# A fused decoder layer with routed experts: the first expert rows are issued behind three weight loads, and the last batch's routing moves one pipeline step

## The chip, the cores and the metric

The kernel runs on one core of one Trainium2 chip. The metric is device microseconds (us) of one execution, the median over runs. The engines are named PE (TensorE, matrix multiplies), DVE (VectorE), ACT (ScalarE), POOL (GpSimd) and SP (SyncE, which here only issues DMAs).

## What is computed

The reference takes `x` of 4 batches x 512 positions x 128 channels in float32 and adds three blocks to it, each behind a layer norm:

```python
x = x + _L0_attn_ref(_layernorm(x), ...)            # gated Toeplitz mixer over four positions
x = x + _L0_xattn_ref(_layernorm(x), ctx_1024, ...) # 16 heads of linear attention on a context of 77
x = x + _L0_ffn_ref(_layernorm(x), router_w, w_gate, w_up, w_down)
```

The third is a mixture of 8 experts, of which each of the 2,048 tokens takes two:

```python
logits = xf @ router_w.T
top_w, top_i = lax.top_k(softmax(logits), 2);  top_w = top_w / top_w.sum(-1)
g, u = xf @ w_gate[e].T, xf @ w_up[e].T        # 128 -> 256, for each expert e
y = (silu(g) * u) @ w_down[e].T                # 256 -> 128
out = sum over the two chosen experts of top_w * y
```

Only the chosen experts need be computed. The layer norm in front of it, the logits, the choice of experts and the combination are all part of the kernel.

## The kernel before

The engines run five instruction streams written out by hand, with semaphores between them. There are three stages one after the other: the mixer, the attention (16 heads on each of four batches of 512 tokens) and the experts.

**Routing.** For each batch m, `third_norm(m)` normalises the tokens into the tile `rows` (128 partitions x 2 choices x 4 tiles x 130 numbers: 128 channels, a token number and a weight). It has a POOL part (`var_eps`, then `rstd`, lines 517 to 523) and a DVE part (line 927). `turn_rows` (PE, line 1038) transposes the rows, `turned_rows` (ACT) copies them to `y3T`, and `router_logits` (PE, line 1187) multiplies them by the router. `routing(m)` is a list of eight DVE pieces: top two of the logits (945, 949), one-hot masks (953, 957), differences (960, 961), then `slots`, `places` and `weights` (965 to 979). `ranks` (PE, lines 1194 to 1202) counts the tokens in front of each token for its expert. `scatter(m, t)` (POOL, line 537) then writes 128 rows to the DRAM tensor `dispatched` (`xs`), at the place of their expert: 4 tiles x 2 choices are eight indirect DMAs for a batch, each adding 16 to the semaphore `sent`.

For batches 0 to 2 all this lies in the attention of the next batch. For batch 3, the last, there is no next attention, so it lies beside the first experts.

**The table of blocks.** The tokens of an expert are cut into blocks of 128. `table_steps` are small DVE steps which turn the counts (`base`) into a table of blocks: where each block's rows start, and so which expert it is. This is done twice: an early table of 16 blocks, built from the first three batches alone (semaphore `table_step` reaches 11), and a late table of 24, with the last batch in it (reaches 32). 39 blocks are run in all.

**Experts.** A block s is loaded by SP: `load_weights(s)` brings the 256 KB of gate and up weights of its expert into one of 8 buffers (`wgu_sb`, line 378) and `load_rows(s)` its 128 rows (65 KB) into one of 16 buffers (`xb`, line 372). `read_rows` reads four or more table entries into SP registers ahead of that (line 367). Rows may be loaded only when the batches they come from have been scattered: SP waits for `sent` of three batches ahead of block 0, and of all four ahead of block 16. Weights of block s from 8 on wait for the gate and up product of block s - 8.

`pipeline(engine, stages, beside)` runs the blocks as software pipeline steps. At step j, PE turns the rows of block j (`turn_x`, line 1242), multiplies block j - 1 by its gate and up weights (`gate_up`, line 1250) and block j - 2 by its down weights (`down`, line 1260). ACT copies the turned rows of block j (line 574), takes the silu of the gate of block j - 1 (`gate`, line 682) and weighs the result of block j - 2 (`weigh`, line 686, tile `yo`). DVE multiplies gate and up (`hidden`, line 1013, block j - 1, tile `hid`). POOL sends the result of block j - 2 by an indirect DMA to `expert_out` (`send`, line 557). Work named under `beside` is written out behind the stages of its step. PE enters this pipeline when DVE is through with all heads of the last batch but one.

After block 38, SP loads `expert_out` back (`y_back`), DVE adds it to X (line 1029) and SP stores X. Each of these waits for every send.

Of the kernel before, what the change touches and what calls it, by code (L numbers as in the profile page):

```python
# [21 lines left out]
NB = 4  # L22
POS = 512
TPB = POS // P
# [20 lines left out]
WRING = 8  # L45
AHEAD = 4
# [11 lines left out]
def decoder_kernel(nc, x, ctxT, wuv, bu, bv, woaT, bo, coef, wk, wv, wq, wo, projT, router, wgu, wd,  # L58
                   out, xs, ys):
    with ExitStack() as ctx:  # L60
# [203 lines left out]
        CONSTS = 18 + RING  # L264

        WARM = 6
        PE_MIXER, PE_Y2, ACT_Y2, DVE_Y2, POOL_LN2 = 2, 6, 6, 3, 2
        POOL_NORM = 3
        SCATTER = (10, 11, 12, 13)
# [33 lines left out]
        def pipeline(eng, stages, window=None, beside=None, late=None, moved=()):  # L303

            depth = max(lag for lag, _ in stages)

            def tick(i, j):  # L310
                for lag, fn in stages:
                    s = i * RING + (j - lag)
                    if 0 <= s < RUN and (fn, s) not in moved:
                        fn(s, (j - lag) % RING, i + (j - lag) // RING, *((j - lag,) if window else ()))
            for i in range(BLOCKS // RING):
                if late and i == EARLY // RING:
                    late()
                if window:
                    window(i)
                for j in range(RING):  # L320
                    tick(i, j)
                    for step in (beside or {}).get(i * RING + j, ()):
                        step()
            if window:
                window(BLOCKS // RING)
            for j in range(depth):
                tick(BLOCKS // RING, j)


        @block.sync  # L330
        def _(sp):
            for g in range(NG):
                part = slice(G // 2 * g, G // 2 * (g + 1))
                sp.dma_start(wk_sb[:, part, :], wk[:, part, :]).then_inc(ld_wk[g], 16)
            for i in range(2):
                part = slice(G * i, G * (i + 1))
                sp.dma_start(wv_sb[:, part, :], wv[:, part, :]).then_inc(ld_wvo[i], 16)
                sp.dma_start(wo_sb[0:DH, part, 0:P], wo[0:DH, part, :]).then_inc(ld_wvo[i], 16)
                sp.dma_start(wo_sb[DH:P, part, P:2 * P], wo[DH:P, part, :]).then_inc(ld_wvo[i], 16)
            sp.dma_start(wuv_sb[:, :], wuv).then_inc(ld_wuv, 16)  # L340
            sp.dma_start(X[:, TPB:2 * TPB, :], x_view[1, :, :, :]).then_inc(ld_x[1], 16)
            for dst, src in ((bias_v[:, :], bv), (bias_u[:, :], bu)):
                sp.dma_start(dst, src).then_inc(ld_bias, 16)
            sp.dma_start(wq_sb[:, :, :], wq).then_inc(ld_wq, 16)
            for n in range(2, NB):
                sp.dma_start(X[:, TPB * n:TPB * (n + 1), :], x_view[n, :, :, :]).then_inc(ld_x[n], 16)
            for dst, src in ((coef_sb[:, :, :], coef), (router_sb[:, :], router)):
                sp.dma_start(dst, src).then_inc(ld_small, 16)
            sp.dma_start(bias_o[:, :], bo).then_inc(ld_biaso, 16)
            sp.dma_start(woa_sb[:, :, :], woaT).then_inc(ld_woa, 16)  # L350

            sp.wait_ge(consts, CONSTS)
            for a in range(0, FILL_ROWS, 43):
                sp.dma_start(xs_blocks[:, a:a + 43, :],
                             pad_row[:, :].unsqueeze(1).broadcast_to([P, 43, ROW])).then_inc(filled, 16)

            sp.wait_ge(wq_lo_done, NG)
            sp.wait_ge(o_full, NB)
            sp.wait_ge(ks_free, UNITS * NB)
            sp.dma_start(wd_sb[:, :, :], wd).then_inc(ld_wd, 16)  # L360

            rows_at = {}
            wgu_rows = wgu.rearrange("e p c -> (e p c)").rearrange("(r c) -> r c", r=E * CAP)

            def read_rows(first, last):
                for s in range(first, last):
                    rows_at[s] = sp.value_load(table[0:1, s:s + 1]).with_bounds(min_val=0, max_val=PAD_ROW)

            def load_rows(s):
                if s >= XRING:  # L370
                    sp.wait_ge(y_sent[s % XRING], s // XRING * 16)
                sp.dma_start(xb[:, s % XRING, :], xs[bass.ds(rows_at[s], P), :]).then_inc(ld_xb[s % XRING], 16)

            def load_weights(s):
                if s >= WRING:
                    sp.wait_ge(gu_full, s - WRING + 1)
                at = (rows_at[s] & ((E - 1) * CAP)).with_bounds(min_val=0, max_val=(E - 1) * CAP)
                sp.dma_start(wgu_sb[:, s % WRING, :], wgu_rows[bass.ds(at, CAP), :].rearrange("(p a) c -> p (a c)", p=P)
                             ).then_inc(ld_wgu[s % WRING], 16)

            sp.wait_ge(table_step, ROWS_EARLY)
            for a in range(0, WRING, AHEAD):
                read_rows(a, a + AHEAD)
                for s in range(a, a + AHEAD):
                    load_weights(s)
            sp.wait_ge(sent, 16 * TOPK * TPB * (NB - 1))
            for s in range(WRING):
                load_rows(s)
            for s in range(WRING, EARLY):
                if s % AHEAD == 0:  # L390
                    read_rows(s, s + AHEAD)
                load_rows(s)
                load_weights(s)

            sp.wait_ge(table_step, ROWS_LATE)
            read_rows(EARLY, EARLY + XRING)
            for s in range(EARLY, EARLY + 2):
                load_weights(s)
            sp.wait_ge(sent, 16 * TOPK * TPB * NB)
            for s in range(EARLY, EARLY + 2):  # L400
                load_rows(s)
            for s in range(EARLY + 2, RUN):
                if s >= EARLY + XRING:
                    read_rows(s, s + 1)
                load_weights(s)
                load_rows(s)

            for j in (*range(RUN % XRING, XRING), *range(RUN % XRING)):
                sp.wait_ge(y_sent[j], len(range(j, RUN, XRING)) * 16)
            for n in range(NB):  # L410
                sp.dma_start(y_back[:, n, :, :].rearrange("p k c -> p (k c)"), ys_view[n, :, :]).then_inc(ld_y[n], 16)
            for n in range(NB):
                sp.wait_ge(add_step, 2 * (n + 1))
                sp.dma_start(out_view[n, :, :, :], X[:, TPB * n:TPB * (n + 1), :]).then_inc(stored, 16)
            sp.wait_ge(stored, 16 * NB)
# [3 lines left out]
        def _(pool):  # L419
# [109 lines left out]
            def scatter(m, t):  # L529

                if t == 0:
                    pool.wait_ge(dest_done, m + 1)
                    pool.sem_inc(waits_passed, 1)
                    wait_alone(pool, y3_twice, m + 1)
                    wait_alone(pool, route, m * ROUTE_STEPS + ROUTE_STEPS + 1)
                for k in range(TOPK):
                    g.indirect_dma_start(  # L537
                        out=xs, out_offset=bass.IndirectOffsetOnAxis(ap=slot_i[:, t, k:k + 1], axis=0),
                        in_=rows[:, k, t, :], in_offset=None).then_inc(sent, 16)
# [18 lines left out]
                    out=ys, out_offset=bass.IndirectOffsetOnAxis(ap=xb[:, s % XRING, P:P + 1].bitcast(I32), axis=0),  # L558
                    in_=yo[:, s % XRING, :], in_offset=None, bounds_check=NO_DEST - 1, oob_is_err=False).then_inc(y_sent[s % XRING], 16)

            pipeline(pool, [(2, send)], beside={5: [lambda t=t: scatter(NB - 1, t) for t in range(TPB)]})


        @block.scalar
        def _(act):
# [118 lines left out]
            def weigh(s, j, turn):  # L684
# [2 lines left out]
                             scale=xb[:, s % XRING, P + 1:P + 2]).then_inc(yo_done, 1)  # L687

            pipeline(act, [(0, keep_x), (1, gate), (2, weigh)], beside={
                2: [lambda: turned_rows(NB - 1)],  # L690
                3: [lambda: second_rows(NB - 1)],
                4: [lambda: second_silu(NB - 1)]})


        @block.vector
        def _(dve):
# [314 lines left out]
            def hidden(s, j, turn):  # L1011
# [2 lines left out]

            part = routing(NB - 1)
            pipeline(dve, [(1, hidden)], beside={
                1: [lambda: third_norm(NB - 1)],
                2: [lambda: table_steps(0, EARLY, WORDS_EARLY, USED)],
                3: part[0:5],
                4: part[5:8],  # L1020
                5: [lambda: table_steps(EARLY, LATE, 0, 4)],
                6: [lambda: table_steps(EARLY, LATE, 4, 9)],
                7: [lambda: table_steps(EARLY, LATE, 9, 13)],
                8: [lambda: table_steps(EARLY, LATE, 13, 16)]})
            for n in range(NB):
                dve.wait_ge(ld_y[n], 16)
                part = X[:, TPB * n:TPB * (n + 1), :].rearrange("p t c -> p (t c)")
# [7 lines left out]
        def _(pe):  # L1035
# [240 lines left out]
            def one_expert(ap):  # L1276
                return ap.rearrange("p a c -> p (a c)")

            pipeline(pe, [(0, turn_x), (1, gate_up), (2, down)], load_experts, beside={
                2: [lambda: turn_rows(NB - 1)],  # L1280
                3: [lambda: router_logits(NB - 1)],
                4: [lambda: ranks(NB - 1)]},
                late=lambda: pe.wait_ge(table_step, WORDS_LATE))


# [38 lines left out]
```

## Time and profile before

| | |
|---|---|
| median of three runs | 284.33 us (284.23 to 286.0) |
| time of the profiled execution | 283.41 us |
| its span in the trace | 281.6 us, so 1.8 us lie around the span |
| mean granted clock of PE | 0.968 of full speed |
| PE busy | 250.0 us (89%) |
| DVE busy | 190.6 us (68%) |
| ACT busy | 163.9 us (58%) |
| POOL busy | 123.7 us (44%) |

All times in rows are us from the start of the span. The attention ends on PE at about 195 us, the experts run from about 199 to 266 us, and the loads back, sums and stores fill the rest. Shares of the whole span do not say much here: what matters is which wait ends last at the seam between attention and experts, and at the seam between block 15 and block 16.

### The profile page before, as it was taken

The page shows a single profiled execution, that of the slowest core. Times are in us where ns is not written, and L with a number is a line of the kernel's source. Part 1 is how long each engine was busy: PE and PEld are TensorE (multiplying, and loading weights), DVE is VectorE, ACT ScalarE, POOL GpSimd, SP SyncE. Part 2 cuts the span into 40 slices and gives each one's busy share as a digit, 9 for nine tenths or more (in the row PEclk, how much of TensorE's full clock was granted, in tenths as well). Part 3 has the DMA queues.
Part 4 walks back from the last instruction along what each step waited for, and adds up shares of the span by engine and source line. Part 5 has one row for each costly group of instructions (what it writes and reads, how often), then busy time and mean ns, then how long its engine had stood idle before and what let it go on. Part 6 is the DMA issues. An engine that isn't in the chain of part 4 may idle for free.

```text
span 281.6 us, 5724 instructions
## 1 busy us (share of the span) xinstructions
PE 250.0 (89%) x1697; PEld 214.2 (76%) x1697; DVE 190.6 (68%) x713; ACT 163.9 (58%) x343; POOL 123.7 (44%) x183
## 2 busy tenths in 40 slices
PE   7799999999999999999998999896799989999700
PEld 4558677676888999879887998775699989999600
DVE  4868759587868888998889889899367222232215
ACT  3566466564677777667766776661156656565400
POOL 5648999651001002047103701270236777777710
PEclk9999999999999999999999999999699999999975
DMA  7999999930012000001000100019557579984147
GB/s 208 276 240 202 204 205 195 198 47 2 0 58 94 0 0 3 1 21 48 9 3 17 52 11 3 9 55 280 155 160 198 160 211 281 354 256 130 43 181 266
DMA packets 38446, 34.05 MB, mean 121 GB/s; under 512 B 3581, under 2 KB 31234, under 8 KB 38288
## 3 DMA queue, kind: packets, MB, share of 16 engines
q1 hardware_dynamic: 35312, 28.96, 43.4%
q0 software_dynamic: 2272, 4.24, 4.4%
q10 hardware_dynamic: 832, 0.49, 0.6%
q8 instruction: 15, 0.25, 0.4%
q14 instruction: 15, 0.12, 0.1%
HBM read 19.80 MB, written 14.32 MB: 121 GB/s over the span
## 4 chain that ended last, share of the span: by engine, by line
PE 59%; DVE 20%; DMA 8%; SPq 5%; issue 4%; POOL 2%; ACT 1%; DVEq 0%; POOLq 0%; ACTq 0%
PE bank L1250 10%; PE num L1175 10%; DVE X L913 8%; PE bank L1136 5%; PE num L1260 5%; PE num L1114 5%; DMA xb<-dispatched 3%; PE num L245 3%; PE num L247 3%; PE bank L245 3%; PE num L246 3%; PE bank L1078 3%; PE bank L246 2%; PE bank L247 2%; DMA wo_sb<-in_wo 2%
## 5 line engine op out<-in xcount | busy, mean ns | idle before, releaser
L913 DVE SCALAR_TENSOR_TENSOR X<-num,rden,X 128x128 f32<-128x128 f32 x256 | 72.1, 344 | 6.6
L1175 PEld LDWEIGHTS num<-kvw_sb,q 128*128 128x128 f32 x512 | 65.9, 190 | 12.0 <-ACT q L574 5.7
L1175 PE MATMUL num<-kvw_sb,q 128*128 128x130 f32 x512 | 68.7, 277 | 3.6 <-DVE X L913 3.6
L657 ACT ACTIVATE relu_z<-bank 128x512 f32<-128x512 f32 x64 | 38.1, 596 | 21.6 <-PE bank L247 21.5
L537 POOL DMA_INDIRECT dispatched<-rows,slot_i x32 | 31.3, 977 | 40.4 <-DVE rows L979 31.6
L557 POOL DMA_INDIRECT expert_out<-yo,xb x39 | 38.1, 977 | 20.1 <-ACT yo L686 11.3
L1013 DVE TENSOR_TENSOR hid<-bank,silu_g 128x256 f32<-128x256 f32 x39 | 16.5, 424 | 41.2 <-ACT silu_g L682 41.2
L574 ACT ACTIVATE q<-relu_z 128x512 f32<-128x512 f32 x64 | 40.4, 632 | 6.7 <-DVE acc L832 0.8
L1250 PE MATMUL bank<-xT,wgu_sb 128*128 128x128 f32 x312 | 43.3, 284 | 0.2 <-ACT xT L574 0.2
L1250 PEld LDWEIGHTS bank<-xT,wgu_sb 128*128 128x128 f32 x312 | 39.8, 200 | 0.5 <-issue 0.5
L245 PE MATMUL bank<-y2T_hi,feat_hi 128*128 128x512 f32 x64 | 30.4, 475 | 0.2
L682 ACT ACTIVATE silu_g<-bank 128x256 f32<-128x256 f32 x39 | 15.0, 384 | 22.0 <-PE bank L1250 21.0
L1260 PE MATMUL num<-wd_sb,hid 128*128 x156 | 24.9, 283 | 0.6 <-ACT yo L686 0.6
L246 PE MATMUL bank<-y2T_lo,feat_hi 128*128 128x512 f32 x64 | 25.1, 392 | 0.0
L247 PE MATMUL bank<-y2T_hi,feat_lo 128*128 128x512 f32 x64 | 25.1, 392 | 0.0
L1260 PEld LDWEIGHTS num<-wd_sb,hid 128*128 128x128 f32 x156 | 20.9, 194 | 0.9 <-issue 0.8
L517 POOL TENSOR_SCALAR var_eps<-moments_b 128x4 f32<-128x4 f32 x4 | 0.9, 229 | 46.9 <-DVE moments_b L922 46.9
L1114 PEld LDWEIGHTS num<-vw,kp 77*128 77x128 f32 x128 | 16.8, 190 | 3.2 <-issue 1.9
L783 DVE TENSOR_SCALAR kp<-num 77x512 f32<-77x512 f32 x16 | 10.9, 679 | 11.0 <-PE num L247 11.0
L574 ACT ACTIVATE vw<-num 77x512 f32<-77x512 f32 x16 | 9.5, 595 | 14.7 <-PE num L247 14.7
L1114 PE MATMUL num<-vw,kp 77*128 77x130 f32 x128 | 16.9, 274 | 0.0
L686 ACT ACTIVATE yo<-num,xb 128x128 f32<-128x128 f32 x39 | 14.3, 368 | 4.4 <-PE num L1260 1.8
(170 smaller groups left out, 403.2 us busy)
## 6 DMA issues: line engine op xcount, KB each, us to landing
wgu_sb<-in_wgu SPq DMA_DIRECT2D x39, 256.0 KB, 3.4
dispatched<-pad_row SPq DMA_DIRECT2D x3, 2795.0 KB, 32.6
xb<-dispatched SPq DMA_DIRECT2D x39, 65.0 KB, 3.5
y_back<-expert_out SPq DMA_DIRECT2D x4, 512.0 KB, 4.9
wd_sb<-in_wd SPq DMA_DIRECT2D x1, 1024.0 KB, 4.7
out<-X SPq DMA_DIRECT2D x4, 256.0 KB, 2.4
X<-in_x SPq DMA_DIRECT2D x3, 256.0 KB, 5.9
expert_out<-yo,xb POOLq DMA_INDIRECT x39, 3.5
```

Of the source, the lines that this page charges most:

```text
L245: nc.tensor.matmul(ps, a_hi, b_hi, start=start, stop=False)
L246: nc.tensor.matmul(ps, a_hi, b_lo, start=False, stop=False)
L247: return nc.tensor.matmul(ps, a_lo, b_hi, start=False, stop=stop)
L537: g.indirect_dma_start(out=xs, out_offset=bass.IndirectOffsetOnAxis(ap=slot_i[:, t, k:k + 1], axis=0), in_=rows[:, k, t, :], in_offset=Non ...
L557: g.indirect_dma_start(out=ys, out_offset=bass.IndirectOffsetOnAxis(ap=xb[:, s % XRING, P:P + 1].bitcast(I32), axis=0), in_=yo[:, s % XRIN ...
L574: return a.activation(dst, src, ACT.Copy, **kw)
L657: a.activation(relu_z[:, k % 2, :], z_bank[k % 2], ACT.Relu).then_inc(relu_done, 1)
L913: v.scalar_tensor_tensor(tile_of(n, t), banks[:, t // 2, t % 2, 0:P], rden[:, h % 2, t:t + 1], tile_of(n, t), ALU.mult, ALU.add).then_inc( ...
L1114: last = nc.tensor.matmul(ks_bank[u % 2][:, HA * i:HA * (i + 1)], kp[:, (u // 2) % 2, M * h:M * (h + 1)], vw[:, (u // 2) % 2, h, :], start ...
L1175: nc.tensor.matmul(num[:, 2 * (h % 2) + t // 2, HA * (t % 2):HA * (t % 2 + 1)], q[:, h % 4, part], kvw_h, start=True, stop=True).then_inc( ...
L1250: last = nc.tensor.matmul(gu_bank[j % 2][:, part], wgu_sb[:, s % WRING, part], xT[:, j % 2, :], start=True, stop=True)
L1260: last = nc.tensor.matmul(dn_bank[j % 2][:, 0:P], hid[:, j % 2, part], one_expert(wd_sb[:, bass.ds(e, 1), part]), start=c == 0, stop=c == 1)
```

## The change

SP's order is changed for the first eight blocks. Before, it was table entries 0 to 3, weights 0 to 3, entries 4 to 7, weights 4 to 7, the wait for `sent`, rows 0 to 7. Now it is entries 0 to 3, weights 0 to 2, entries 4 to 7, the wait for `sent`, rows 0 and 1, and then weights 3, rows 2, weights 4, rows 3 and so on up to weights 7, rows 6, rows 7. What is issued up to rows 7 is the same in number.

On PE, ACT, DVE and POOL, everything of the last batch's routing that stands beside the expert pipeline moves one step later: the norm, the turning, the logits, the ranks, the late table and the scatters.

```diff
+        FIRST = 3
...
             sp.wait_ge(table_step, ROWS_EARLY)
-            for a in range(0, WRING, AHEAD):
-                read_rows(a, a + AHEAD)
-                for s in range(a, a + AHEAD):
-                    load_weights(s)
+            read_rows(0, AHEAD)
+            for s in range(FIRST):
+                load_weights(s)
+            read_rows(AHEAD, WRING)
             sp.wait_ge(sent, 16 * TOPK * TPB * (NB - 1))
-            for s in range(WRING):
+            for s in range(FIRST - 1):
                 load_rows(s)
+            for s in range(FIRST, WRING):
+                load_weights(s)
+                load_rows(s - 1)
+            load_rows(WRING - 1)
...
-            pipeline(pool, [(2, send)], beside={5: [lambda t=t: scatter(NB - 1, t) for t in range(TPB)]})
+            pipeline(pool, [(2, send)], beside={6: [lambda t=t: scatter(NB - 1, t) for t in range(TPB)]})
...
             pipeline(act, [(0, keep_x), (1, gate), (2, weigh)], beside={
-                2: [lambda: turned_rows(NB - 1)],
-                3: [lambda: second_rows(NB - 1)],
-                4: [lambda: second_silu(NB - 1)]})
+                3: [lambda: turned_rows(NB - 1)],
+                4: [lambda: second_rows(NB - 1)],
+                5: [lambda: second_silu(NB - 1)]})
...
             pipeline(dve, [(1, hidden)], beside={
-                1: [lambda: third_norm(NB - 1)],
-                2: [lambda: table_steps(0, EARLY, WORDS_EARLY, USED)],
-                3: part[0:5],
-                4: part[5:8],
-                5: [lambda: table_steps(EARLY, LATE, 0, 4)],
+                2: [lambda: third_norm(NB - 1)],
+                3: [lambda: table_steps(0, EARLY, WORDS_EARLY, USED)],
+                4: part[0:5],
+                5: part[5:8],
+                6: [lambda: table_steps(EARLY, LATE, 0, 4)],
...
             pipeline(pe, [(0, turn_x), (1, gate_up), (2, down)], load_experts, beside={
-                2: [lambda: turn_rows(NB - 1)],
-                3: [lambda: router_logits(NB - 1)],
-                4: [lambda: ranks(NB - 1)]},
+                3: [lambda: turn_rows(NB - 1)],
+                4: [lambda: router_logits(NB - 1)],
+                5: [lambda: ranks(NB - 1)]},
```

SP's queue before, from the weights of block 6 to the rows of block 1 (the waits of an instruction stand in brackets):

```order
L378 REGISTER_ALU
L378 ISA
L378 DMA wgu_sb<-in_wgu 128x512
L378 REGISTER_ALU
L378 ISA
L378 DMA wgu_sb<-in_wgu 128x512
L372 ISA [waits sent]
L372 DMA xb<-dispatched 128x130
L372 ISA
L372 DMA xb<-dispatched 128x130
```

SP's queue in the changed kernel, from the weights of block 2 to the weights of block 3 (its lines are five or fewer numbers further down):

```order
L379 REGISTER_ALU
L379 ISA
L379 DMA wgu_sb<-in_wgu 128x512
L368 TENSOR_LOAD table x4
L373 ISA [waits sent]
L373 DMA xb<-dispatched 128x130
L373 ISA
L373 DMA xb<-dispatched 128x130
L379 REGISTER_ALU
L379 ISA
L379 DMA wgu_sb<-in_wgu 128x512
```

Five weight loads that stood ahead of the first rows now stand behind them, one between each two rows.

PE before, from the gate and up products of block 1 to those of block 2 (`num<-ident,xb` turns a block's rows, `bank<-ident,rows` turns the last batch's rows for the router):

```order
L1250 MATMUL bank<-xT,wgu_sb 128x128 x4
L1260 REGISTER_ALU
L1260 ISA
L1260 MATMUL num<-wd_sb,hid 128x128
L1260 ISA
L1260 MATMUL num<-wd_sb,hid 128x128
L1038 MATMUL bank<-ident,rows 128x128 x4
L1242 MATMUL num<-ident,xb 128x128
L1250 MATMUL bank<-xT,wgu_sb 128x128 x4
```

PE in the changed kernel, from the turning of block 3's rows to that of block 4's:

```order
L1247 MATMUL num<-ident,xb 128x128
L1255 MATMUL bank<-xT,wgu_sb 128x128 x4
L1265 REGISTER_ALU x2
L1265 ISA
L1265 MATMUL num<-wd_sb,hid 128x128
L1265 ISA
L1265 MATMUL num<-wd_sb,hid 128x128
L1043 MATMUL bank<-ident,rows 128x128 x4
L1247 MATMUL num<-ident,xb 128x128
```

The turning of the last batch's rows stood behind the down product of block 0, and now stands behind that of block 1.

DVE before, at the start of the expert pipeline:

```order
L1013 TENSOR_TENSOR hid<-bank,silu_g 128x256
L927 TENSOR_SCALAR rows<-X,moments_b,rstd 128x128 x4
L1013 TENSOR_TENSOR hid<-bank,silu_g 128x256
L896 TENSOR_TENSOR t_start<-t_end,t_nb 1x8
L897 TENSOR_SCALAR t_tmp<-t_end 1x8
```

DVE in the changed kernel, at the same place:

```order
L1018 TENSOR_TENSOR hid<-bank,silu_g 128x256 x2
L932 TENSOR_SCALAR rows<-X,moments_b,rstd 128x128 x4
L1018 TENSOR_TENSOR hid<-bank,silu_g 128x256
L901 TENSOR_TENSOR t_start<-t_end,t_nb 1x8
L902 TENSOR_SCALAR t_tmp<-t_end 1x8
```

The norm of the last batch is now behind the products of blocks 0 and 1, and not behind that of block 0 alone. On POOL, in the same way, five sends stand ahead of the eight scatters where there were four, and 34 behind them where there were 35.

## Rows read from the trace of the kernel before

**Rows 1.** The page's granted clock of PE in 40 slices of the span, tenths of full speed

```profile
PEclk9999999999999999999999999999699999999975
```

**Rows 2.** Windows: stretch and length; busy us and count by engine; clock, DMA

```profile
core 0: us, PE busy (x) PEld busy (x) DVE busy (x) ACT busy (x) POOL busy (x), PEclk, DMA share, GB/s
...
195.30:198.80 3.50, 0.02 (x1) 0.00 (x0) 3.04 (x16) 0.00 (x0) 0.19 (x1) 0.99 0.94 283
198.80:205.50 6.70, 6.40 (x29) 6.11 (x30) 2.38 (x11) 1.80 (x7) 1.25 (x3) 0.50 0.46 107
...
226.80:232.70 5.90, 4.63 (x40) 4.41 (x39) 1.57 (x4) 3.13 (x10) 4.68 (x5) 1.00 0.86 251
```

**Rows 3.** Chain that ended last, 186 to 201 us: start, length, what

```profile
190.43 0.33 SPq L378
...
191.38 0.29 SPq L367
...
192.28 0.28 SPq L367
...
195.05 3.76 DMA xb<-dispatched
```

**Rows 4.** Timeline, 186 to 201 us: start, length, instruction, idle time before it

```profile
189.68 0.96 POOL L537 DMA_INDIRECT dispatched<-rows,slot_i  x1 [0.30 <-issue]
...
194.75 1.13 DVE L913 SCALAR_TENSOR_TENSOR X<-num,rden,X 128x128 f32<-128x128 f32 x4
...
198.13 0.38 DVE L922 BATCH_NORM_AGGREGATE moments_b<-stats 128x2 f32<-128x6 f32 x4
...
198.99 1.04 POOL L522 TENSOR_TENSOR rstd<-var_eps,p_mhalf 128x4 f32<-128x4 f32 x1
```

**Rows 5.** Timeline of PE, 193.9 to 206 us

```profile
198.85 0.69 PE L1242 MATMUL num<-ident,xb 128*128 128x128 f32 x2 [3.53 <-DMA xb<-dispatched]
199.78 2.05 PE L1250 MATMUL bank<-xT,wgu_sb 128*128 128x128 f32 x8 [0.25 <-ACT xT L574]
...
205.25 0.42 PE L1242 MATMUL num<-ident,xb 128*128 128x128 f32 x1
```

**Rows 6.** Timeline of DVE, 195.9 to 204 us: the last batch's norm

```profile
202.63 1.11 DVE L927 TENSOR_SCALAR rows<-X,moments_b,rstd 128x128 f32<-128x128 f32 x4
```

**Rows 7.** Timeline, 216 to 226 us: a step at full clock

```profile
216.47 1.06 PE L1250 MATMUL bank<-xT,wgu_sb 128*128 128x128 f32 x8
...
217.57 0.39 ACT L682 ACTIVATE silu_g<-bank 128x256 f32<-128x256 f32 x1 [0.47 <-PE bank L1250]
...
217.95 1.06 PE L1250 MATMUL bank<-xT,wgu_sb 128*128 128x128 f32 x8
217.99 0.42 DVE L1013 TENSOR_TENSOR hid<-bank,silu_g 128x256 f32<-128x256 f32 x1 [0.49 <-ACT silu_g L682]
```

**Rows 8.** Chain that ended last, 175 to 282 us: the seam at block 16

```profile
222.88 2.85 DMA dispatched<-rows,slot_i
225.88 0.33 SPq L372
...
228.60 4.09 DMA xb<-dispatched
```

**Rows 9.** Timeline of PE, 224.9 to 229.5 us: the rows of block 16

```profile
226.20 0.63 PE L1260 MATMUL num<-wd_sb,hid 128*128 x4
227.79 0.33 PE L1242 MATMUL num<-ident,xb 128*128 128x128 f32 x1 [0.96 <-DMA xb<-dispatched]
```

**Rows 10.** Timeline, 208 to 282 us: first scatter of the last batch; last weighing and last send

```profile
214.04 0.96 POOL L537 DMA_INDIRECT dispatched<-rows,slot_i  x1 [0.30 <-issue]
...
266.26 0.37 ACT L686 ACTIVATE yo<-num,xb 128x128 f32<-128x128 f32 x1 [0.97 <-PE num L1260]
...
267.58 0.97 POOL L557 DMA_INDIRECT expert_out<-yo,xb  x1 [0.30 <-issue]
```

More of the change, by code:

```diff
@@ L1016, in _ @@
             pipeline(dve, [(1, hidden)], beside={
-                1: [lambda: third_norm(NB - 1)],
-                2: [lambda: table_steps(0, EARLY, WORDS_EARLY, USED)],
-                3: part[0:5],
-                4: part[5:8],
-                5: [lambda: table_steps(EARLY, LATE, 0, 4)],
-                6: [lambda: table_steps(EARLY, LATE, 4, 9)],
-                7: [lambda: table_steps(EARLY, LATE, 9, 13)],
-                8: [lambda: table_steps(EARLY, LATE, 13, 16)]})
+                2: [lambda: third_norm(NB - 1)],
[3 more added lines that the diff above has]
+                6: [lambda: table_steps(EARLY, LATE, 0, 4)],
+                7: [lambda: table_steps(EARLY, LATE, 4, 9)],
+                8: [lambda: table_steps(EARLY, LATE, 9, 13)],
+                9: [lambda: table_steps(EARLY, LATE, 13, 16)]})
             for n in range(NB):
```

## The prediction

> **What bounds the kernel now.** I began with the granted clock. It is full through the attention and falls in one slice in the middle, just behind it [rows 1]. The windows show why that slice is worth a look: from 195.3 to 198.8 us PE is busy for 0.02 of 3.5 us, and in the 6.7 us behind that it runs at 0.50 of its clock, 1.2 and not 2.4 GHz [rows 2]. The chain that ended last names what PE waited for there. SP issues weights 2 at 190.43, reads four table entries from 191.38 to 192.56, issues more weights, and only at 195.05 the rows of block 0, which take 3.76 us to land [rows 3]. PE idles 3.53 us for them [rows 5]. The rows need not be that late: PE's own gate into the experts is that DVE is through with all heads but one, which is at 194.75 + 1.13 = 195.88 [rows 4].
>
> A second seam has to be passed on. The rows of block 16 wait for the last batch's scatters. The last scatter leaves at 222.88 and has landed 2.85 us later, SP issues rows 16 at 225.88 [rows 8], and PE turns them at 227.79, after 0.96 us of waiting [rows 9]. So the end of the kernel hangs on the routing of the last batch, and whatever PE saves before block 16 only lengthens the 0.96 us, unless that routing comes earlier too. Behind block 16 PE runs nearly without a gap up to the last weighing at 266.26, and the last send starts at 267.58 [rows 10].
>
> **The change, part by part.** *Rows 0 on SP.* Between 190.43 and 195.05 lie six weight loads (2 to 7) and four table reads. The reads take 192.56 - 191.38 = 1.18 us, so a load costs (4.62 - 1.18) / 6 = 0.57 us. With three loads ahead, rows 0 can go at 190.43 + 0.57 + 1.18 = 192.2. They also need the scatters of batch 2: the last of them left at 189.68 [rows 4], and with the 2.85 us of the later last scatter [rows 8] it has landed at 192.5. The two meet, and I take 192.6 for the issue. Landing: rows 16 were turned 1.91 us after their issue (225.88 to 227.79) [rows 8, 9]; the longest in that stretch took 4.09 us [rows 8]. Eight weight loads stood ahead of the 3.76 us of rows 0, and three stand there now, of which the first two have had three us to pass. I take 2 us, so rows 0 land at 194.6. At 4.09 they would land at 196.7.
>
> PE then starts at its gate, 195.88 plus some 0.1, say 195.98. **First term: 195.98 - 198.85 = -2.87 us.**
>
> *Rows 2 and on.* At 0.57 us an issue, rows 2 leave at 192.6 + 3 x 0.57 = 194.3, and each further block 1.14 us later. At 2 us they land at 196.3 and at 4.09 us at 198.4. PE wants them at 197.8 (below), so the middle of these bounds costs nothing and the far end 0.6 us. Weights 3 leave at 193.8 instead of 191.0, and are wanted by the fourth product, after 201 us: hidden by three steps, and worth nothing unless they took 7 us. Rows 7 end on SP after as many instructions as before, so what is queued behind them (rows 8, and weights 8, which wait for the first product) does not slip.
>
> *The clock and the step.* PE's idle time ahead of rows 0 shrinks from 3.53 us to about 0.7 (195.3 to 195.98). A gap of 0.96 us at the later seam left the clock at 1.00 [rows 2, 9]. I take the full clock. The Trainium skill, in TensorE: Matmul & The Clock Gate (Part 1, the HAM clock gate), says that half rate is the default, that activity releases it and that idle time brings it back; this trace agrees, with 0.50 behind 3.53 us of idling. By that rule the same mechanism could strike at block 16, which is a rival below.
>
> The stretch from PE's start to the end of the turning of the last batch's rows is 205.25 - 198.85 = 6.40 us before [rows 5]. After, it holds one step more, but at full clock. The first products began 0.93 us after the start [rows 5]; a transpose less slow makes it 0.73, so 196.7. A block's products are 1.06 us and a step 217.95 - 216.47 = 1.48 us at full clock, where they took 2.05 at half clock [rows 5, 7]. So the second products run from 197.9 (behind the turning of rows 2 at 197.8) to 198.95. ACT's silu follows the products by 0.04 us and takes 0.39, DVE's product follows and takes 0.42 [rows 7]: DVE has block 1 at 199.85. Block 0's is sooner, though not before DVE's sums for the last batch end at 198.51 [rows 4]. The norm is now behind block 1. It also needs `rstd` of POOL, done at 198.99 + 1.04 = 200.03 [rows 4]. So it starts at 200.05 and not at 202.63, and with its 1.11 us [rows 6] ends at 201.2. That one block more in front of it costs nothing, because POOL's `rstd` is not sooner; without that cover it would cost a step. Four transposes of some 0.12 us behind each other, the latency of the handover, and the turning is over by 201.8. **Second term: (201.8 - 195.98) - 6.40 = -0.58 us.** Together -3.45 us at this point, and PE has the products of one block more behind it.
>
> *From there to block 16.* The order of logits, ranks, table and scatters against the blocks around them is the same as before, each with a block number one higher, and before too this stretch ran at full clock (0.50 ends at 205.5) [rows 2]. The first scatter was at 214.04 behind four sends [rows 10]; now five sends stand ahead, the fifth for a block which PE finishes where it finished the fourth. The eight scatters and the wait of SP for them are unchanged, and the late table moves with them. So everything down to rows 16 comes 3.4 us sooner. **Third term: 0.** PE itself reaches rows 16 a step sooner still, so its 0.96 us there grow to 0.96 + 1.48 = 2.4 us, all idle.
>
> *Behind block 16.* 23 blocks, with the same loads in front: 0. One send fewer is left behind the scatters. The last weighing ended at 266.63 and the last send left 0.95 us later [rows 10]; POOL may win some 0.1 us here, which I leave out. Loading back, sums and stores are unchanged.
>
> **Sum:** -2.87 - 0.58 + 0 = -3.45, which I round to -3.4 us. The profiled execution took 283.41 us, so its like would take 280.0. The median of the runs is 284.33, 0.9 above it, and with 3.4 taken off that is **280.9 us**.
>
> **Rivals.** *A. The clock falls at block 16.* The new gap of 2.4 us lies between 0.96 us, which left the clock alone, and 3.53 us, which halved it [rows 2, 9]. If it falls, 6.7 us of work at half clock go as 3.35 at full clock would: +3.35 us, and the kernel ends at 280.9 + 3.35 = 284.3. For it speaks that 2.4 is nearer to 3.53 than to 0.96; against it, that PE would be fully busy on both sides. [...] Chance 0.10.
>
> *B. The front is won only in part.* Rows 2 land at the far bound and later ones queue behind the weights between them, or the clock falls all the same in the thinner stretch behind 195.3. In half clock the steps go as before: the stretch of 6.40 us and one step more at half clock, some 2.05 us, is 8.45 from 195.98, which ends at 204.4 and not 205.25: -0.8 us, 283.5. Late rows alone, 1 to 2 us, give 282 to 283. For it speaks that the DMA engines are 0.94 busy up to 198.8 [rows 2], and that rows among weights took 4.09 us [rows 8]; against it, that nobody sends results in this stretch. In DMA: Bandwidth & Descriptors (Queues, rings and completion order) the Trainium skill says that on each DMA engine one issuer's descriptors are taken in ring order, so a weight load put ahead of a row load is paid by the row load. By it rows 0 gain five loads, and rows 2 to 7 each stand behind the weights issued just ahead of them. Chance 0.20.
>
> *C. Slower.* Rows 0 do not land sooner: the four table reads and the scatters of batch 2 hold SP, or the landing takes what it took. Then only the second part of the change is left. The last batch's norm waits for one step more, at half clock (2.05 us), and rows 16 come as much later: 284.33 + 2.05 = 286.4. It decides from the point where PE starts less than 2.05 us sooner and the clock still falls, which is a start after 196.8. Against it stands that rows 0 would have to take over 4.2 us from 192.6. Chance 0.07.
>
> **How the numbers follow.** My forecast has 0.63, with a range of its own of 280.0 to 281.9: the landing of rows 2 at its bounds, the start, and POOL's part. A has 0.10, B 0.20 and C 0.07. A change of under 1%, 2.8 us, is about what a measurement of this kernel can not tell from none, so faster means below 281.5 us. That takes five sixths of my forecast and a little of B: 0.55. The rest of the forecast, A and nearly all of B are within 1%: 0.37. Slower by over 1% is C and a tail: 0.08. The range that leaves out less than 2 in 10 goes from 279.9 to A's 284.4.
>
> **What would show it.** In the profile of the changed kernel: SP's first row load at 192.2 to 192.9; PE's first transpose of `xb` at 195.9 to 196.1 with an idle time under 1 us; no slice below full clock near 200 us; the norm at 200.0 to 200.5, right behind `rstd`; the first scatter of the last batch near 210.6; PE waiting some 2.4 us for rows 16, and turning them near 224.4 at full clock. A first transpose after 196.8, or a clock of 0.5 behind either seam, would make me wrong.

## The result, and the profile after

In 20 runs of each kernel in turn, the changed kernel takes 282.78 us (281.37 to 284.53) where the kernel before took 284.74 (282.89 to 288.02). The ratio is 0.9923, with a 95% interval of 0.9900 to 0.9946: faster by 2.2 us, between 1.5 and 2.8 (the two medians alone differ by 2.0). The prediction said 3.4 us and 280.9. The profiled execution took 281.58 us (before 283.41).

The granted clock tells the first half of the story. This is the page's row of the changed kernel, in 40 slices as [rows 1]:

```profile
span 279.8 us, 5724 instructions
...
PEclk9999999999999999999999999999999979999965
```

The dip behind the attention is gone, and there is a new one further on, in the slice from 224 to 231 us, behind the seam at block 16. The windows of the changed kernel, with the columns of [rows 2], show both places:

```profile
198.80:205.50 6.70, 6.58 (x60) 6.40 (x59) 4.28 (x22) 4.52 (x13) 3.63 (x6) 1.00 0.81 201
222.70:225.50 2.80, 0.00 (x0) 0.00 (x0) 0.28 (x1) 0.28 (x1) 2.19 (x3) 1.00 0.33 95
225.60:226.30 0.70, 0.70 (x7) 0.70 (x8) 0.00 (x0) 0.28 (x1) 0.58 (x1) 1.00 0.79 252
226.40:229.70 3.30, 3.30 (x18) 3.30 (x17) 0.42 (x1) 0.92 (x3) 2.61 (x3) 0.50 0.89 278
```

From 198.8 to 205.5 PE works through 60 matmuls and not 29. From 222.7 to 225.5 it does nothing, waiting for the rows of block 16. Behind that it runs at full clock for 0.7 us and then at half clock for the 3.3 us of the fourth row.

Before single instructions are compared, one correction is due. The code up to the end of the attention is the same, but its time is not. The last but one head is finished on DVE (the gate that lets PE into the experts) in the row that starts at 194.75 before [rows 4] and at 195.41 after:

```profile
195.41 1.13 DVE L918 SCALAR_TENSOR_TENSOR X<-num,rden,X 128x128 f32<-128x128 f32 x4
```

In the profiles of this study on undisturbed chips that start lies between 194.62 and 198.35 us, whatever the kernel. So I count from this start, and call it G. The instructions that the prediction named, in the changed kernel's timeline:

```profile
197.19 0.41 PE L1247 MATMUL num<-ident,xb 128*128 128x128 f32 x2 [1.20 <-issue]
...
200.87 1.11 DVE L932 TENSOR_SCALAR rows<-X,moments_b,rstd 128x128 f32<-128x128 f32 x4
...
211.24 0.96 POOL L542 DMA_INDIRECT dispatched<-rows,slot_i  x1 [0.31 <-issue]
...
225.53 0.33 PE L1247 MATMUL num<-ident,xb 128*128 128x128 f32 x1 [2.96 <-DMA xb<-dispatched]
```

| from G, us | before | after | difference |
|---|---|---|---|
| PE turns rows 0 | 198.85 - 194.75 = 4.10 | 197.19 - 195.41 = 1.78 | -2.32 |
| last batch's rows turned, next block begins | 10.50 | 202.63 - 195.41 = 7.22 | -3.28 |
| first scatter of the last batch | 19.29 | 15.83 | -3.46 |
| PE turns rows 16 | 33.04 | 30.12 | -2.92 |
| end of the span | 86.83 | 84.39 | -2.44 |

At the first scatter of the last batch the gain is whole. It loses 0.5 us up to rows 16 and another 0.5 behind them. The 2.44 us agree with the 2.2 of the timed runs.

### The profile page after: what moved, and what is told of

It is laid out like the page before. It is cut to its first block, busy times and chain, and to the rows that moved or that the text cites. A ratio compares the mean times of both kernels' runs of the same rounds, so it can differ in the third digit from the quotient of the medians.

```text
span 279.8 us, 5724 instructions
## 1 busy us (share of the span) xinstructions
PE 249.0 (89%) x1697; PEld 213.0 (76%) x1697; DVE 190.6 (68%) x713; ACT 163.7 (58%) x343; POOL 124.2 (44%) x183
## 4 chain that ended last, share of the span: by engine, by line
PE 59%; DVE 22%; DMA 6%; issue 5%; POOL 4%; SPq 1%; ACT 1%; DVEq 0%; POOLq 0%; ACTq 0%
PE num L1180 11%; DVE X L918 10%; PE bank L1255 9%; PE bank L1141 5%; PE num L1119 5%; PE num L1265 5%; PE num L245 3%; PE num L247 3%; PE bank L245 3%; PE num L246 3%; PE bank L1083 3%; PE bank L246 2%; PE bank L247 2%; DMA wo_sb<-in_wo 2%; POOL expert_out L562 2%
## 5 line engine op out<-in xcount | busy, mean ns | idle before, releaser
L1255 PE MATMUL bank<-xT,wgu_sb 128*128 128x128 f32 x312 | 42.6, 281 | 0.3 <-ACT xT L579 0.3
L1255 PEld LDWEIGHTS bank<-xT,wgu_sb 128*128 128x128 f32 x312 | 39.0, 196 | 0.6 <-issue 0.6
```

The costliest lines, as they stand in the source:

```text
L1255: last = nc.tensor.matmul(gu_bank[j % 2][:, part], wgu_sb[:, s % WRING, part], xT[:, j % 2, :], start=True, stop=True)
```

## The experiments

All ratios are against the kernel before, timed in turn on the same chip. The last four columns are from one profiled execution of each kernel: G is a time from the start of the span, and the other three are us from G.

| kernel | ratio (95%) | G | first scatter | rows 16 | end |
|---|---|---|---|---|---|
| before | 1 | 194.75 | 19.29 | 33.04 | 86.83 |
| changed | 0.9923 (0.9900 to 0.9946) | 195.41 | 15.83 | 30.12 | 84.39 |
| changed, second profile (a3) | 0.9883 (0.9838 to 0.9928) | 194.62 | 16.78 | 31.12 | 85.48 |
| rows only (e1) | 0.9942 (0.9906 to 0.9978) | 197.12 | 15.62 | 29.45 | 83.08 |
| step only (e2) | 1.0083 (1.0041 to 1.0124) | 197.50 | 19.61 | 33.64 | 87.60 |
| matmuls in the gap (e3) | 0.9893 (0.9837 to 0.9949) | 196.42 | 15.82 | 29.94 | 83.38 |
| scatters at step 5 (e4) | 0.9895 (0.9831 to 0.9959) | 195.74 | 14.29 | 28.34 | 81.86 |
| rows only, scatters at 4 (e7) | 0.9829 (0.9788 to 0.9870) | 196.31 | 14.11 | 28.84 | 83.19 |
| e4 and the word first (e8) | 0.9817 (0.9776 to 0.9859) | 196.81 | 14.07 | 28.67 | 81.89 |
| changed, rows 16 first (e9) | 0.9971 (0.9933 to 1.0008) | 197.12 | 15.83 | 29.43 | 87.08 |
| e8, rows 16 first (e10) | 0.9850 (0.9791 to 0.9910) | 198.35 | 14.59 | 27.84 | 83.25 |

**One half of the change at a time.** First only SP's order, with everything under `beside` at its old step:

```diff
-                2: [lambda: third_norm(NB - 1)],
+                1: [lambda: third_norm(NB - 1)],
```

> Only SP's new order, with the last batch's routing at its old steps. Theory 1 (the norm is held by POOL's rstd at about 200.7 us in either kernel, so the step moved buys nothing and makes PE idle one step longer at block 16): the last batch's rows are turned at about 202.4, the first scatter leaves at about 211, rows 16 are turned within 0.4 us of where the changed kernel turned them (225.6), PE idles there 1.4 to 1.7 us and not 2.95, and the clock stays at 1.00: 1.0 to 1.5 us faster than the changed kernel, about 3.3 us under the kernel before. Theory 2 (the step is needed, since the product of block 1 now waits behind the norm on DVE): the stretch up to the turning takes longer and the first scatter is later than 211.2; 281 us or more against 284.3, no better than the changed kernel.

In its timeline the norm waits for POOL's `rstd`, and PE for the norm (0.99 us) and later for rows 16:

```profile
202.44 1.12 DVE L932 TENSOR_SCALAR rows<-X,moments_b,rstd 128x128 f32<-128x128 f32 x4 [0.77 <-POOL rstd L527]
...
226.57 0.33 PE L1247 MATMUL num<-ident,xb 128*128 128x128 f32 x1 [0.91 <-DMA xb<-dispatched]
```

Theory 1 had the order of the waits right: the norm is held by `rstd`, and the step isn't needed. Two of its numbers were off: PE idles 0.91 us at the seam (2.96 in the changed kernel) and not 1.4 to 1.7, and rows 16 come 0.67 us sooner from G than in the changed kernel, not within 0.4. The first scatter is 0.2 us sooner from G than with the step, and the clock stays up. From G to the end it is 1.3 us faster than the changed kernel. The median doesn't show that: its ratio of 0.9942 overlaps the changed kernel's from above. So from the profiles the step moved buys nothing; timed, the two can't be told apart.

The other half alone:

```diff
+            for a in range(0, WRING, AHEAD):
+                read_rows(a, a + AHEAD)
+                for s in range(a, a + AHEAD):
+                    load_weights(s)
```

> Only the routing of the last batch one step later, SP's order as before. Both theories agree that this alone costs: PE still waits 3.5 us for the first rows and runs at half clock behind them, and the norm waits one step at half clock. By rival C of the prediction rows 16 come 2.05 us later, and the kernel is 2.0 us slower than before. If the norm's step is hidden by POOL after all, it would be within 0.5 us of before.

It is 2.4 us slower by the ratio (1.2 to 3.5), which holds rival C's price of 2.05 us. The profiled execution is milder: rows 16 come 0.60 us later from G than before, and the end 0.77 us. The norm waits for two products, but at a clock that is half for a part of the time only. Its mean granted clock is 0.970, and six of the twelve timed runs have 0.953 to 0.958, so others probably spent longer at half clock; no profile shows one of them.

```profile
201.80:206.40 4.60, 4.47 (x22) 4.12 (x23) 0.42 (x1) 1.42 (x5) 1.14 (x2) 0.63 0.45 120
231.20:234.00 2.80, 2.80 (x25) 2.80 (x26) 0.42 (x1) 1.34 (x5) 2.18 (x3) 1.00 0.84 234
```

The second row is behind this kernel's own seam at block 16: PE had idled 2.71 us there and kept the full clock.

**What the clock costs at block 16.** Matmuls whose result nobody reads fill a part of the gap:

```diff
+        FILL = 5
...
+            def filler():
+                for i in range(FILL):
+                    nc.tensor.matmul(t_bank, feat_hi[:, 0:M], y2T_hi[:, 0, :], start=True, stop=True)
...
+                15: [filler]},
```

> The changed kernel with five extra matmuls (128x512 columns, about 0.4 us each, into a PSUM bank that nobody reads) behind step 15 on PE, where it waits for the rows of block 16. They do extra work whose result is not used. Theory 1 (the granted clock falls for want of PE activity there, and that costs): the clock stays at 1.00 behind block 16, nothing else moves, and the kernel is 1.1 to 1.7 us faster than the changed one, so 3.3 to 3.9 under before. Theory 2 (behind block 16 the loads are the bound and the half clock is hidden): the clock stays up, and PE waits for the rows of blocks 18 and 19 instead; within 0.4 us of the changed kernel.

The five took 1.39 us together and left 1.62 us idle. The clock stays at 1.00:

```profile
223.34 1.39 PE L1287 MATMUL bank<-y2T_hi,feat_hi 128*128 128x512 f32 x5
226.36 0.33 PE L1248 MATMUL num<-ident,xb 128*128 128x128 f32 x1 [1.62 <-DMA xb<-dispatched]
...
231.22 0.33 PE L1248 MATMUL num<-ident,xb 128*128 128x128 f32 x1 [0.26 <-DMA xb<-dispatched]
```

```profile
226.40:229.70 3.30, 3.30 (x30) 3.30 (x31) 0.64 (x2) 1.74 (x6) 2.69 (x3) 1.00 0.87 256
```

These are 30 matmuls where the changed kernel got through 18 in the same 3.3 us. From rows 16 to the end it takes 83.38 - 29.94 = 53.44 us, and the changed kernel 54.27 (54.36 in its second profile, where the clock fell again). Against e3 that is 0.8 to 0.9 us for the clock, under the 1.1 to 1.7 expected. These are single profiles, and the others with full clock and no long wait there have 53.24 (e8), 53.52 (e4), 53.63 (e1), 53.79 (before) and 53.96 (e2), so the price lies anywhere from 0.3 to 1.1 us. A part is hidden: at full clock PE waits 0.26 us for the rows of block 19, at half clock it doesn't. The timed ratio, 0.9893, points the same way, but its interval overlaps that of the changed kernel. The clock itself shows in the timed runs too: its mean is 0.976 to 0.981 in all six of e3, and 0.974 or less in 16 of the 20 of the changed kernel. So it is shown that the clock falls for want of work on PE; what that costs is shown only roughly.

**Who holds the scatters.** POOL sends four results and not five ahead of them:

```diff
-            pipeline(pool, [(2, send)], beside={6: [...scatter...]})
+            pipeline(pool, [(2, send)], beside={5: [...scatter...]})
```

> The changed kernel with the last batch's scatters behind the fourth send on POOL (step 5) and not the fifth (step 6). The routing was done at 208.9 and the first scatter left at 211.24. Theory 1 (the fifth send, not the routing, holds the scatters): the first scatter leaves at 209.2 to 209.5, rows 16 are turned about 1.9 us sooner (223.8), PE idles there about 1.1 us, the clock stays at 1.00: 2.5 to 3.3 us faster than the changed kernel. Theory 2 (POOL's sends at the end are the bound, since one more of them is left behind the scatters): no more than 0.5 us faster than the changed kernel.

```profile
210.03 0.96 POOL L542 DMA_INDIRECT dispatched<-rows,slot_i  x1 [1.02 <-DVE rows L984]
224.08 0.33 PE L1247 MATMUL num<-ident,xb 128*128 128x128 f32 x1 [1.16 <-DMA xb<-dispatched]
```

Now the scatters wait for the routing itself. Rows 16 come 1.78 us sooner from G than in the changed kernel, the gap is 1.16 us, the clock stays, and from G to the end it is 2.5 us faster. The first scatter is 14.29 us from G where 13.8 to 14.1 were expected: POOL issues it 0.79 us behind the end of the routing at 209.24. The timed ratio gives 0.8 us and not 2.5, with intervals that overlap, and the profiled execution was the fastest of the six. How much this kernel is faster is therefore open; where its scatters wait is not.

**A disturbed chip.** Three kernels ran on a chip where the kernel before took 315.5 us: the changed kernel again (a2, ratio 0.9847, 0.9782 to 0.9912), SP's new order with scatters at step 4 (e5, 1.0024, 0.9984 to 1.0064), and scatters at step 5 with PE's word load first (e6, 0.9931, 0.9891 to 0.9971).

> The changed kernel itself once more, as the base for the others on the same chip and as a second look at the seam. Theory 1 (PE idles there about 2.9 us, and whether the clock falls depends on how that idle time meets the moment at which activity is looked at): in most runs the mean granted clock shows some 3.4 us more at half rate than the version with extra matmuls, in a few none. 0.99 to 0.995 of before, end of the attention gate to the end of the kernel 84.0 to 84.6 us where the clock falls and 83.4 to 83.7 where it doesn't.

> Only SP's new order, routing at its old steps, and the scatters one step before their old place (behind three sends, step 4). Theory 1 (the norm is bound by POOL's rstd, the scatters by the end of the routing, and the step is not needed at all): the first scatter leaves 14.0 to 14.3 us behind the end of the next to last head on DVE (in the changed kernel 15.8), PE waits less than 0.4 us for rows 16, the clock stays up, and from that head to the end of the kernel it takes 82.0 to 82.5 us against the changed kernel's 84.4: 0.984 to 0.987 of before. Theory 2 (the step buys time for the norm): 83 us or more, no better than 0.99.

> The kernel with the scatters at step 5, and PE's load of the first experts' word ahead of its wait for the attention instead of behind it. In the changed kernel PE turned rows 0 only 0.65 us behind its gate, with no DMA named as the cause. Theory 1 (that time is the register load and what PE's sequencer does behind the wait): the first transpose comes 0.1 to 0.2 us behind the gate, 0.5 us sooner; rows 16 only 0.1 to 0.3 us sooner, as the norm waits for POOL's rstd; 0.1 to 0.3 us faster than with the scatters alone. Theory 2 (rows 0 land only then): the first transpose stays at 0.65 us behind the gate.

Engines stood still there with no work or DMA named as the cause, among them DVE for 9.75 us, with PE waiting up to 6.7 us for it. From the waits of the first of them (us in total, times, longest):

```profile
DVE hid L1018 <- issue: 24.0, 13, 9.8
```

What held them I can't say, and only one place of these three is used below, PE's entry into the experts. The same three kernels follow from an undisturbed chip, as a3, e7 and e8.

> The changed kernel again, on another chip than the one on which the kernel before took 315.5 us. If that chip alone was disturbed, the kernel before takes 284 to 285 us here and this one 0.99 to 0.995 of it. Theory 1 (idling of PE ahead of rows 16 makes the clock fall in most executions, at 0.8 us): PE idles 2.7 to 3.2 us there; with the clock fallen 54.0 to 54.4 us from the turning of rows 16 to the end, without 53.4 to 53.7.

Here rows 16 come 1.0 us later from G than in the first profile, and the first scatter is 0.95 us later already. A rival of the prediction is at work, rows of an early block landing late. PE waits for those of block 3, and the turning of the last batch follows:

```profile
200.84 0.33 PE L1247 MATMUL num<-ident,xb 128*128 128x128 f32 x1 [0.73 <-DMA xb<-dispatched]
225.74 0.47 PE L1247 MATMUL num<-ident,xb 128*128 128x128 f32 x1 [2.98 <-DMA xb<-dispatched]
```

> Only SP's new order, routing at its old steps, scatters one step ahead of their old place (behind three sends). The same kernel as the one that ran on the disturbed chip. Theory 1 (the step buys nothing): first scatter 14.0 to 14.3 us behind the end gate of the attention, against the 15.8 of the changed kernel and the 14.3 of the one with scatters at step 5; PE waits under 0.4 us for rows 16; 0.984 to 0.988 of before. Theory 2 (the step buys time): no better than 0.99.

The old steps with scatters one step ahead reach rows 16 with 0.30 us of waiting, then lose 1.39 us at the rows of block 19, which SP's loads don't bring in time. Timed it is at 0.9829, and the changed kernel beside it at 0.9883, with intervals that overlap a little. So without the step, and with the scatters pulled ahead, the kernel is at least no slower.

**PE's entry into the experts.**

```diff
             pe.wait_ge(table_step, WORDS_EARLY)
-            pe.wait_ge(att_done, (NB * H - 1) * TPB)
-            pe.wait_ge(ld_wd, 16)
...
             def load_experts(i):
                 words[:] = [pe.value_load(word_of[0:1, bass.ds(w, 1)]) ...]
+                if i == 0:
+                    pe.wait_ge(att_done, (NB * H - 1) * TPB)
+                    pe.wait_ge(ld_wd, 16)
```

> The changed kernel with scatters at step 5 and PE's word load ahead of its wait for the attention. On the disturbed chip the first transpose came 0.06 us behind its gate. Expected here: the same, rows 16 turned 0.2 to 0.4 us sooner against the gate than with the scatters alone (28.3 us), and 0.982 to 0.987 of before: the fastest of all.

```profile
197.99 0.44 PE L1245 MATMUL num<-ident,xb 128*128 128x128 f32 x2 [0.60 <-DVE X L918]
```

PE turns rows 0 at G + 1.18 us where it was G + 1.78, 0.06 us behind its gate (196.81 + 1.12 = 197.93). With the load behind the wait it was 0.65. Rows 16 did not come sooner than in e4 (28.67 us from G against 28.34), though 0.2 to 0.4 us sooner were expected. From G, the norm, which now waits 0.34 us for `rstd`, is 0.14 us sooner, the first scatter 0.22 and SP's load of rows 16 0.50. But that load took 3.02 us to land where it took 2.18 in e4 (the first row is of e4, the second of e8):

```profile
221.85 2.18 DMA xb<-dispatched
...
222.42 3.02 DMA xb<-dispatched
```

Its 280.54 us and 0.9817 are the lowest of all, but e7 beside it can't be told from it, and its interval still touches that of the changed kernel.

**The landing of the last scatter.** The chain of the changed kernel has 3.36 us where [rows 8] has 2.85; its second profile has 3.42:

```profile
220.09 3.36 DMA dispatched<-rows,slot_i
```

```diff
-            for s in range(EARLY, EARLY + 2):
-                load_weights(s)
             sp.wait_ge(sent, 16 * TOPK * TPB * NB)
             for s in range(EARLY, EARLY + 2):
                 load_rows(s)
+                load_weights(s)
```

> The changed kernel, with the weight loads of blocks 16 and 17 behind the row loads of blocks 16 and 17 on SP instead of ahead of them. In two looks at the changed kernel the last scatter took 3.36 and 3.42 us to land, before it took 2.85. Theory 1 (those 512 KB of weights, issued within the last microseconds ahead of the last scatter, share the DMA engines with it): it lands in 2.3 to 2.7 us, and from its issue to the turning of rows 16 it takes 4.2 to 4.6 us and not 5.4; PE then waits about 2.2 us. Weights 16 land about 3 us behind their issue, at about the time PE wants them, so it gains at most 0.8 us, and may give it back. Theory 2 (the landing varies on its own or by the sends): 3.2 to 3.5 us again.

> The fastest version so far (scatters at step 5, word load first) with the same exchange of rows 16, 17 and weights 16, 17. Theory 1: 0.3 to 0.8 us faster than the 81.9 us it took from the attention gate to the end, if weights 16 are in time. Theory 2: within 0.3 us, or slower because weights 16 are late for their product.

```profile
221.79 2.73 DMA dispatched<-rows,slot_i
```

```profile
232.88 0.47 PE L1246 MATMUL num<-ident,xb 128*128 128x128 f32 x1 [2.69 <-DMA xb<-dispatched]
```

With those two weight loads out of its way the scatter lands in 2.73 us (2.46 in e10), where theory 1 said 2.3 to 2.7. That fits theory 1 but doesn't show it. Before and in e1, e2 and e3 weights 16 are issued 0.9 to 1.1 us ahead of the last scatter, as in the changed kernel, and it took 2.85, 2.95, 3.24 and 3.29 us. In e4, e7 and e8 they are issued 0.3 to 0.8 us behind it, and it took 2.83, 3.48 and 2.54. e8 and e10 differ by this exchange alone, and by 0.08 us. The landing varies by more than the exchange moves it.

But three weight loads are now issued within 1.7 us ahead of the rows of block 18, which take 5.38 us to land. PE waits 2.69 us for them, and the kernel loses more than it won: 0.9971, against 0.9923 and 0.9883. In e10 that wait is 1.70 us. Neither is an improvement. Behind the 2.69 us of e9 the granted clock falls again, for 3.4 us:

```profile
232.90:236.20 3.30, 3.30 (x16) 3.30 (x17) 0.42 (x1) 0.91 (x3) 2.39 (x4) 0.52 0.98 287
```

## Why the prediction came out as it did

- **What bounds the kernel:** right. Rows 0 were the cause of both the idling and the half clock behind it. Both went together in e1, and both stayed in e2.
- **First term, PE starts 2.87 us sooner:** it was 2.32. PE's gate was taken as the start with 0.1 us on top. What failed is that 0.1: PE loads a word of the table behind its wait, which the 3.53 us of idling had covered. It took 0.65 us, and e8 brought 0.06. Rows 0 also left later than I said (G - 1.41 us against G - 2.15). SP issued them 3.66 us behind the last scatter of batch 2 (190.34 to 194.00), for which I had allowed 2.9. That cost nothing, since they landed ahead of PE's gate all the same.
- **Second term, -0.58 us:** it was -0.96 (5.44 against 6.40 us). As I had reckoned, the end of this stretch hangs on `rstd` and not on PE's start: it came 7.22 us from G where 7.05 were foretold, and PE's late start only shortened the stretch. So 0.38 of the 0.55 us lost in the first term came back here. The norm started 0.18 us behind the end of `rstd` (199.65 + 1.04 = 200.69), so the cover that I named was nearly exactly as long as the step put in front of it. The two terms together are -3.28, foretold -3.45.
- **Third term, everything down to rows 16 moves alike:** right up to the last scatter (-3.46 at the first), wrong by 0.5 us behind it. I took the landing of the last scatter over from before, as if it were fixed. It took 3.36 and 3.42 us and not 2.85. In the eleven profiles on undisturbed chips it lies between 2.46 and 3.48 us. The weights of blocks 16 and 17 may be a part of that, but e9 doesn't show it, and the cause is open.
- **Behind block 16, 0:** it was +0.48. Rival A, which I gave 0.10, happened, in both profiles of the changed kernel. Its mechanism and place were right, and e3 shows it. Its price of 3.35 us was not: the half clock lasted 3.4 us and not 6.7, and a part lay under the wait for block 19. It measured 0.8 to 0.9 us against e3 and 0.48 against the kernel before. I had taken PE's idling there as 2.4 us; with the late landing it was 2.96. Whether 2.4 us would have kept the clock is open: in e9 2.25 us kept it.
- **Rival B:** its late rows were seen twice, as waits of 0.73 us (a3) and 0.53 us (e10) for the rows of block 3. **Rival C:** its price of 2.05 us lies within the timed 1.2 to 3.5 us of e2, but e2's profile has rows 16 only 0.60 us later, so the price isn't shown. It was misread too: 2.05 us is what the products of one block took at half clock [rows 5]. A whole step is 1.48 us at full clock, so my estimate for one at half clock should have been 2.96 us.
- **The signs:** of those named ahead, the norm, the first scatter and the full clock near 200 us came true, counted from G. The issue of rows 0, PE's first transpose and the idle time at rows 16 missed. The clock of 0.5 behind block 16 did appear, by which, in the prediction's own words, it was wrong there.
- **The chances:** a gain of 0.77% is within 1%, to which I gave 0.37, and not over it, to which I gave 0.55. The 282.78 us lie outside the forecast's own range of 280.0 to 281.9 and inside the wide one only because that reached up to rival A, whose price was wrong. The own range left no room for three losses of one sign: the word load, the landing and the clock.

The Trainium skill's rule on the clock, in TensorE: Matmul & The Clock Gate (Part 1), that idle time of PE brings the half rate back, agrees with both seams: 0.50 behind 3.53 us of idling before, and 0.50 behind 2.96 us in the changed kernel. What the runs add is that the length of the idle time alone doesn't decide: 2.71 us (e2) kept the full clock and 2.69 us (e9) lost it.

## What to carry to other kernels

When a wait of an engine is taken away, list what that engine did within the wait. It comes to light next: here it was a register load of 0.65 us. A duration that was read once, such as the landing of a scatter, is no constant either, and needs a range of its own. When work upstream is sped up more than the wait downstream, the idle time only moves, and on PE it may take the clock down at its new place, as the 2.96 us here did; so pull the downstream chain (here the scatters, one step sooner on POOL) by as much.

## What the runs showed of the hardware

- A register load and what belongs to it, behind a semaphore wait, kept PE from its first matmul for 0.65 us (0.06 us in e8, with the load ahead of the wait).
- PE at half clock came back to full after 3.4 us at the seam of block 16, in e9's wait for block 18 and at e2's first seam, and after 6.7 us at the first seam of before.
- Idle times of nearly one length on PE left the clock full (2.71 us, e2) or took it down (2.69 us, e9).
- The last indirect scatter of 128 rows landed in 2.46 to 3.48 us. What makes the difference isn't shown.
- The same code up to the last head but one of the attention took 194.6 to 198.4 us in different executions on undisturbed chips. What varies there was not looked into. It is more than this change is worth, and only counting from a common instruction made single profiles comparable.
- One chip ran the same programs 11% slower, with engines standing still between instructions for up to 9.75 us.
